# Row numbers of a routed block computed one block further ahead in a decoder layer's expert stage

## The reference

```
x      = layernorm(x).reshape(1024, 256)
shared = silu_and_mul(x @ shared_gate_up_w.T) @ shared_down_w.T     # 704 hidden
shared = shared * sigmoid(x @ sgate_w.T)
weights = softmax(x @ gate_w.T)                                     # 16 experts
topk_w, topk_ids = top_k(weights, 4)
for e in range(16):
    coef = sum(where(topk_ids == e, topk_w, 0), -1)
    h    = silu_and_mul(x @ w13[e].T)                               # 2 x 176
    acc += (h @ w2[e].T) * coef[:, None]
out = shared + acc
```

## Time and profile before

| what | value |
|---|---|
| median of three runs | 344.32 us |
| profiled execution, its own time | 343.41 us |
| span in its profile, first to last instruction | 341.6 us |
| PE busy, PEld, DVE, ACT, POOL | 308.8, 238.2, 241.5, 186.7, 146.6 us |
| the block loop, from the first `turn_block` to the last `block_down` | 196.75 to about 314 us |
| after the loop | about 314 to 341.6 us |

### The profile page before, as it was taken

One profiled execution on the slowest core, in us unless ns is written; L12 is line 12 of the kernel. 1 busy time (PEld: TensorE's weight loads), 2 busy tenths in 40 slices (PEclk: granted clock), 3 DMA queues, 4 the chain that ended last, 5 costly groups with the idle time before them and its releaser, 6 DMA issues.

```text
span 341.6 us, 8504 instructions
## 1 busy us (share of the span) xinstructions
PE 308.8 (90%) x2606; PEld 238.2 (70%) x2608; DVE 241.5 (71%) x720; ACT 186.7 (55%) x538; POOL 146.6 (43%) x179
## 2 busy tenths in 40 slices
PE   6897899999999997879997789998999989999983
PEld 2354576667667764658775578787978979888862
DVE  2357788988888799563887856576766666765396
ACT  1052889888898977473697333343434434342231
POOL 3584133544544413487578253333434434345000
PEclk9999999999999998996999989999999999999998
DMA  7997197989899941023122526777777777774681
GB/s 210 302 389 307 25 310 179 302 248 291 242 264 266 239 141 33 16 98 113 54 94 96 157 66 187 214 218 233 209 230 210 220 224 213 229 220 149 249 319 61
DMA packets 44153, 66.84 MB, mean 196 GB/s; under 512 B 5347, under 2 KB 31988, under 8 KB 43604
## 3 DMA queue, kind: packets, MB, share of 16 engines
q1 hardware_dynamic: 39476, 54.91, 55.0%
q0 software_dynamic: 3792, 10.56, 8.1%
q10 hardware_dynamic: 848, 0.92, 1.2%
HBM read 37.07 MB, written 29.30 MB: 194 GB/s over the span
## 4 chain that ended last, share of the span: by engine, by line
PE 53%; DVE 9%; DMA 8%; issue 8%; SPq 8%; POOL 7%; ACT 6%; DVEq 0%; ACTq 0%; POOLq 0%
PE bank L1524 16%; PE bank L1802 6%; DMA xb<-x_slots 6%; POOL x_slots L538 5%; PE bank L1441 5%; PE bank L1450 5%; ACT probs L650 4%; PE bank L1394 3%; PE bank L1459 3%; SPq L425 3%; PE bank L1772 2%; SPq L432 2%; PE bank L1483 2%; PE bank L1792 2%; PE bank L1562 2%
## 5 line engine op out<-in xcount | busy, mean ns | idle before, releaser
L613 POOL DMA_INDIRECT y_picks<-yb,ids x47 | 45.1, 960 | 70.0 <-DVE yb L1285 69.4
L650 ACT ACTIVATE probs<-bank,neg_max 128x128 f32<-128x128 f32 x256 | 70.7, 399 | 2.7 <-DVE neg_max L903 2.5
L1802 PE MATMUL bank<-w,hbt 128*128 128x256 f32 x188 | 48.3, 380 | 0.0
L903 DVE TENSOR_REDUCE neg_max<-bank 128x4 f32<-128x512 f32 x64 | 42.1, 683 | 5.8 <-PE bank L1441 5.7
L1450 PE MATMUL bank<-ident,probs 128*128 128x128 f32 x256 | 36.9, 281 | 2.6 <-ACT probs L650 2.6
L812 ACT ACTIVATE xbt_h<-bank 128x256 fp32r<-128x256 f32 x47 | 18.0, 384 | 38.5 <-PE bank L1772 38.4
L538 POOL DMA_INDIRECT x_slots<-x,slots x32 | 34.5, 1080 | 9.3 <-issue 8.9
L1450 PEld LDWEIGHTS bank<-ident,probs 128*128 128x128 f32 x256 | 29.1, 143 | 12.4 <-ACT probs L650 10.3
L1802 PEld LDWEIGHTS bank<-w,hbt 128*128 128x128 f32 x188 | 32.1, 190 | 2.5
L1278 DVE TENSOR_TENSOR hb<-sg,bank 128x176 f32<-128x176 f32 x47 | 15.9, 337 | 24.0 <-ACT sg L820 24.0
L820 ACT ACTIVATE sg<-bank 128x176 f32<-128x176 f32 x47 | 14.9, 317 | 30.2 <-PE bank L1524 30.2
(11 more groups left out here) (175 smaller groups left out, 677.6 us busy)
## 6 DMA issues: line engine op xcount, KB each, us to landing
x_slots<-zero_b SPq DMA_DIRECT2D x16, 1072.0 KB, 10.9
w<-w_in_dram SPq DMA_DIRECT2D x47, 256.0 KB, 3.1
xb<-x_slots SPq DMA_DIRECT2D x47, 134.0 KB
w<-w_in_dram SPq DMA_DIRECT2D x4, 1408.0 KB, 12.6
yg<-y_picks SPq DMA_DIRECT2D x8, 512.0 KB, 7.0
sw_raw<-shared_in_dram SPq DMA_DIRECT2D x6, 384.0 KB, 3.4
ktc<-keys_in_dram SPq DMA_DIRECT2D x8, 256.0 KB, 3.2
ctx_sb<-ctx_in_dram SPq DMA_DIRECT2D x1, 1024.0 KB, 12.6
```

The lines of the kernel that those rows point to most:

```text
L613: pool.indirect_dma_start(y_picks[:, :], bass.IndirectOffsetOnAxis(ids[:, n:n + 1], 0), yb[:, n % RB, :], None).then_inc(yb_placed[n % RB] ...
L650: ins = act.activation(probs[:, g, j, :], ps_s[kind][g][:, 128 * j:128 * j + 128], ACT.Exp, bias=neg_max[:, kind, g, j:j + 1])
L903: dve.tensor_reduce(neg_max[:, kind, g, :], ps_s[kind][g].rearrange("p (j n) -> p j n", j=BLK), AX.X, ALU.max, negate=True).then_inc(max_r ...
L1802: ins = pe.matmul(ps_yb[n % 2][:, 0:D], hbt[:, n % 2, k, :], w2[:, n % RB, k, :], start=k == 0, stop=k == KC - 1)
```

## The change

In DVE's program, `block_ids` moves one block ahead of where it stood. `block_ids(0)` and `block_ids(1)` come before the loop and before `block_hidden(0)`, and turn n of the loop holds `block_ids(n + 2)` where it held `block_ids(n + 1)`. The count of instructions on every engine stays as it was (DVE has 630 rows before and after), and the other four engines' programs are not touched.

```diff
             low_rows_t(0)
             low_rows_t(1)
+            block_ids(0)
+            block_ids(1)
             block_hidden(0)
-            block_ids(0)
             for n in range(NBLK):
                 if n + 2 < NBLK:
                     low_rows_t(n + 2)
                 if n + 1 < NBLK:
                     block_hidden(n + 1)
-                if n + 1 < NBLK:
-                    block_ids(n + 1)
+                if n + 2 < NBLK:
+                    block_ids(n + 2)
                 if n >= 1:
                     take_block(n - 1)
```

## The result

The changed kernel takes 341.06 us, the median of 18 runs (337.77 to 343.31); the kernel before, beside it on the same chip, 343.40 (18 runs, 340.05 to 346.07). The ratio is 0.9942, with a 95% interval of 0.9914 to 0.9969: faster by 2.0 us, the interval reaching from 1.1 to 3.0. The medians take in every run, the ratios leave out runs more than 1.5% above the fastest of their kernel, so a ratio need not be the quotient of two medians. The forecast was 339.9, a gain of 4.4; the time lies in the range, the gain is about half. That the time comes within 1.2 us of the forecast is in part luck: the forecast started from 344.32, the median of three runs of the kernel before, and 18 runs put that kernel at 343.40, 0.9 lower without any change. The profiled execution took 339.67 us (span 337.8), against 343.41 (341.6) before.

A forecast was written before the change was run, and what follows sets the result against it. PE was taken as held up by late row loads, issued only after the row numbers freed their buffer. Removing 4.9 us of stalls, less 0.5 for late loads, gives 4.4: 344.32 becomes 339.9 us, range 338.6 to 343.0.

The forecast's parts named there:

- What bounds the loop: Loop: PE's transposes wait for rows issued late because row numbers hold the buffer; 4.9 us of stalls.
- The two rivals by which nothing would change: Loop: loads were in time anyway (0.02), or SP waits for `block_down` instead and lead stays (0.06); both 344.3 us.
- First step, a lead of 4.69 set by `block_down`: Loop: row loads' lead over their transposes grows from 3.41 to 4.69 us, covering the longest load, 4.30.
- The wait on L432: Loop: SP's wait for PE's `block_down` before a weight load was to grow from 1.4 to several us.
- Second step, the start: Before the loop: earlier row numbers let SP enter some 2.3 us ahead; the first `hb` starts 0.3 us late.
- The cover of 1.26: Loop's start: 1.26 us between the first `hb`'s end and its reader `turn_hidden(0)` were to cover the 0.3 us delay.
- Third step, "SP just keeps up": Loop's end: SP issues the last row load at 298.5; with 4.30 it lands 302.8, PE arriving at 302.6.
- the head start: Loop's start: SP was to issue the rows of block 6 at about 204.5 in place of 206.82, some 2.3 us sooner.
- the 0.5 taken off for late loads: Loop: 0.5 us deducted from the 4.9 us gain for one or two loads meeting a slow stretch of SP.
- The first rival, loads that get slower,: Loop: earlier loads slow down and miss the 4.69 us lead; half the gain, 2.2 us, 342.1; chance 0.17.
- The slower rival: Loop: transfers become the bound; row loads of 5.7 us make the period 2.60, costing 8 us, 352; chance 0.05.

The follow-up runs named there:

- the short SP: SP takes expert numbers from packed words by shift and mask, not a table read per block: 0.9921 on the kernel before, 0.9856 on the changed kernel.

## Why the prediction was half right

*What bounds the loop.* Right. PE waited for rows that were issued late, and the row numbers held them: with the buffer free a block sooner, by the change or by a fifth buffer, 7.8 and 7.1 us of waits become 3.3, 3.5 and 2.4. With the short SP it is 3.6 against 0.3 and less. The two rivals by which nothing would change fall with that.

*First step, a lead of 4.69 set by `block_down`.* The limit is where the prediction put it, but the kernel stays there only with a shorter SP (4.96 on average). In the changed kernel the lead is 4.33 at block 6, 4.24 at block 20, 3.20 at block 41, and in its second execution it starts at 3.68. The wait on L432, expected at several us, came to 1.8.

*Second step, the start.* Half right. `ids` of block 0 was to end at 200.3 and ended at 199.05 + 1.40 = 200.45, and the rows of block 4 went 0.80 later, at 201.25. But the second group ended at 202.49 rather than 201.0, so rows of block 6 went at 205.56 and not at 204.5. The first `hb` started 202.41 - 200.78 = 1.63 us after its input (last section), not 0.3. The cover of 1.26 was used up: PE stood 0.39 us for it.

*Third step, "SP just keeps up".* This is where the size went wrong. SP's pace itself held: the prediction's numbers give (90.8 + 3.2)/40 = 2.35 us a block, and 2.335 was measured up to block 41. But I tested only the last block, against a load of 4.30, and the sum then went by a lead of 4.69 all through. By the prediction's own numbers the last row load goes at 298.5 and PE is there at 302.6, which is a lead of 4.1; and the head start was 1.26 us by the clock (205.56 for 206.82) and not 2.3, which leaves 3.0. What SP loses it doesn't get back while PE runs: 2.335 against 2.303 us a block takes 1.13 us off the lead by block 41, and then a load of 4.83 is late. The second execution entered with 208.74 - 205.06 = 3.68 us at block 6 and had ten late landings of at most 0.7 us, where the first had five with one of 1.9.

So the term that was mis-sized is the 0.5 taken off for late loads: on average of two executions 1.8 us are left. The forecast of 4.4 loses 1.3 there. It loses 0.4 because there was less to save (4.5 on average of two, not 4.9), and 0.3 to 0.4 more at the first `hb`. The 2.3 that remain are what the medians show; with PE's own gaps as uneven as they are, that the sum fits so closely is chance.

*The first rival, loads that get slower,* priced half the gain at 2.2 us, and the size fits; the mechanism doesn't. Its sign, a load of 4.7 us and more on the chain, came once, the 4.83, and that load met a lead of 3.2. The other late loads of both executions took 4.25 us or less and would have fitted into 4.69. The median load was 2.9 us before and 2.9 and 3.0 in the two executions after. With the short SP it does grow, to 3.2, and even there the lead of about 5 covers nearly all. *The slower rival* fell with it.

Open: why SP takes some issues 0.3 us longer with nothing waited for, at the same places of its program, why single loads take over 4 us, and why PE's own gaps vary from 0.5 to 2.9 us between executions.

## What to carry to other kernels

A lead is a balance, not a size: beside the limit that sets it, compare the supplier's and the consumer's own pace over many rows and not over two neighbours: a few slow steps of 0.3 to 0.4 us, which two neighbouring rows don't show, used up 1.1 us in 35 blocks. When two limits lie close together, taking one away pays only up to the other, so price the second before the first (here the queue engine's table read, 0.4 us a block). And where early work is moved to an engine's start, read what the neighbouring engine does in those very microseconds.

## What the runs showed of the hardware

The small DVE instructions of `block_ids` stand still beside POOL. Timeline of DVE after, at the loop's start:

```profile
198.40 0.42 DVE L1290 SCALAR_TENSOR_TENSOR found<-xb,of_block 128x8 f32<-128x8 f32 x1
...
199.05 1.40 DVE L1294 SCALAR_TENSOR_TENSOR ids<-offset,dump 128x1 uint32<-128x1 f32 x1
...
200.37 1.73 DVE L1290 SCALAR_TENSOR_TENSOR found<-xb,of_block 128x8 f32<-128x8 f32 x1
...
202.33 0.16 DVE L1294 SCALAR_TENSOR_TENSOR ids<-offset,dump 128x1 uint32<-128x1 f32 x1
202.41 0.33 DVE L1278 TENSOR_TENSOR hb<-sg,bank 128x176 f32<-128x176 f32 x1
```

POOL beside it, three instructions of 1.65 us each:

```profile
197.12 4.96 POOL L606 TENSOR_TENSOR w_l<-w,w_h 128x704 fp32r<-128x704 f32 x3 [8.31 <-DVE hid_l L1179]
```

ACT, which makes the first `hb`'s input, and PE, which waits for `hb`:

```profile
200.46 0.32 ACT L820 ACTIVATE sg<-bank 128x176 f32<-128x176 f32 x1 [3.51 <-PE bank L1525]
```

```profile
202.80 0.44 PE L1793 MATMUL bank<-ident,hb 128*128 128x128 f32 x2 [0.39 <-DVE hb L1278]
```

`ids` of block 0 ends at 200.45 and `found` of block 1 at 202.10; POOL's second instruction ends at about 200.43 and its third at 202.08. Each DVE instruction is let go when a POOL instruction ends. When POOL was moved, the same instructions took 0.21 and 0.16 us, and those of block 2, now beside POOL, 1.28 and 1.39. In the kernel before, `found` of block 0 started at 200.97 and ended at 201.28, just as POOL's splits ended at 201.25:

```profile
196.31 4.94 POOL L606 TENSOR_TENSOR w_l<-w,w_h 128x704 fp32r<-128x704 f32 x3 [5.64 <-DVE hid_l L1179]
```

The duration that the prediction carried to the earlier place, 0.70 for a group, was thus that of a place where POOL was just done; there it took 200.45 - 198.40 = 2.05. `xbt_l` and `hb`, with one operand in PSUM, are not held: in the run in which POOL waits they start at 199.83 and 201.53, inside POOL's stretch, and take 0.43 and 0.34 us. Nor is the reduction between `found` and `ids`, with one operand: it starts there at 203.10 and takes 0.16.

The Trainium skill, page "SBUF — State Buffer", section "Who interferes with whom", says that a VectorE instruction with two SBUF inputs contends with a GpSimd instruction that reads SBUF and calls the pair of ports that the two share an exclusive lock. The trace agrees, with 1.28 to 1.73 us in place of 0.16 to 0.22. The prediction did not weigh this rule, and it bore on the change.

By rows of the short SP, a weight load's issue takes 0.69 us after the row load's, against 1.11: reading one number from the table costs SP about 0.4 us more than a shift and a mask.
